# Order of work at the passage from attention to feed-forward in a transformer kernel

## The reference

```python
q = (query @ Wq + bq)   # 16 heads of 32; query = layernorm(x), x is (2, 2048, 512)
k = (key_value @ Wk + bk); v = (key_value @ Wv + bv)   # context (2, 77, 384)
attn = softmax(clip(einsum('bhqd,bhkd->bhqk', q, k) * scale, -CLAMP, CLAMP))
x = x + einsum('bhqk,bhkd->bqhd', attn, v) @ Wo + bo
# feed-forward: U1 (512,128), V1 (128,2048), U2 (2048,128), V2 (128,512)
P = layernorm(x) @ U1
H = gelu(P @ V1 + b1)
x = x + (H @ U2) @ V2 + b2
```

## Time and profile before

| | us |
|---|---|
| median of 3 runs | 556.8 |
| lowest and highest | 556.72, 557.4 |
| the profiled execution | 556.77 |
| its span | 555.0 |
| PE busy | 546.0 (98%) |
| DVE busy | 474.7 (86%) |
| POOL busy | 371.7 (67%) |
| ACT busy | 310.3 (56%) |

### The profile page before, as it was taken

One profiled execution on the slowest core, in us unless ns is written; L12 is line 12 of the kernel. 1 busy time (PEld: TensorE's weight loads), 2 busy tenths in 40 slices (PEclk: granted clock), 3 DMA queues, 4 the chain that ended last, 5 costly groups with the idle time before them and its releaser, 6 DMA issues.

```text
span 555.0 us, 12058 instructions
## 1 busy us (share of the span) xinstructions
PE 546.0 (98%) x4824; PEld 464.6 (84%) x4824; DVE 474.7 (86%) x692; ACT 310.3 (56%) x523; POOL 371.7 (67%) x295
## 2 busy tenths in 40 slices
PE   8999999999999999999999999999999999999996
PEld 8997889888988898889877777888888888888885
DVE  5789989888988898889899568989889898978694
ACT  4655454545554555454455546757575757666563
POOL 1788776778777877786679356747484756565581
PEclk9999999999999999999999999999999999999999
DMA  8432452321223122243322230031221222101012
GB/s 320 173 84 75 122 225 93 97 93 64 94 96 109 49 95 97 89 146 129 134 67 75 71 114 1 19 107 46 63 89 58 76 75 79 57 19 58 20 57 94
DMA packets 25551, 50.36 MB, mean 91 GB/s; under 512 B 2968, under 2 KB 3096, under 8 KB 25112
## 3 DMA queue, kind: packets, MB, share of 16 engines
q1 hardware_dynamic: 25208, 49.07, 26.0%
q10 hardware_dynamic: 288, 0.52, 0.3%
HBM read 32.49 MB, written 16.78 MB: 89 GB/s over the span
## 4 chain that ended last, share of the span: by engine, by line
PE 86%; DVE 7%; POOL 3%; ACT 2%; issue 1%; DVEq 0%; POOLq 0%
PE bank L1044 50%; PE ps_s L1044 15%; PE bank L1122 6%; PE ps_s L1096 5%; PE bank L1138 5%; PE bank L1065 2%; PE bank L1169 2%; DVE once L867 1%; PE bank L1204 1%; DVE ssum L835 1%; POOL wqo_r L411 1%; POOL ss L422 1%; DVE wqo_r L872 1%; DVE hs_r L890 1%; POOL ss L430 1%
## 5 line engine op out<-in xcount | busy, mean ns | idle before, releaser
L513 POOL TENSOR_TENSOR hs_r<-ss,hs_r 128x512 fp32r<-128x512 f32 x63 | 88.2, 1401 | 91.4 <-ACT hs_r L743 91.4
L656 ACT ACTIVATE ss<-ps_s,once 128x512 f32<-128x512 f32 x128 | 88.1, 689 | 65.1 <-PE ps_s L1044 61.6
L1044 PE MATMUL ps_s<-p1t_r,v_r 128*128 128x512 f32 x384 | 111.1, 398 | 0.0
L1044 PE MATMUL bank<-hs_r,u_r 128*128 128x512 f32 x381 | 107.2, 390 | 0.0
L1044 PE MATMUL bank<-zt_r,wqo_r 128*128 128x256 f32 x768 | 97.7, 283 | 0.2 <-ACT qt L544 0.2
L422 POOL TENSOR_TENSOR ss<-ss,smax 128x1232 f32<-128x1232 f32 x32 | 74.8, 2338 | 33.0 <-DVE smax L830 33.0
L1044 PE MATMUL bank<-wqo_r,ot_r 128*128 128x512 f32 x384 | 95.5, 398 | 0.0
L1044 PEld LDWEIGHTS bank<-zt_r,wqo_r 128*128 128x128 f32 x768 | 91.8, 188 | 1.5 <-issue 0.4
L1044 PEld LDWEIGHTS bank<-hs_r,u_r 128*128 128x128 f32 x381 | 71.4, 188 | 15.7 <-DVE hs_r L890 0.2
L1044 PEld LDWEIGHTS bank<-wqo_r,ot_r 128*128 128x128 f32 x384 | 69.8, 188 | 13.5 <-DVE ot_r L843 0.2
L1044 PEld LDWEIGHTS ps_s<-p1t_r,v_r 128*128 128x128 f32 x384 | 69.8, 188 | 13.4 <-issue 0.4
(11 more groups left out here) (97 smaller groups left out, 818.1 us busy)
## 6 DMA issues: line engine op xcount, KB each, us to landing
xs<-in_x SPq DMA_DIRECT2D x64, 256.0 KB, 3.4
y_between<-xs SPq DMA_DIRECT2D x32, 256.0 KB, 2.0
fw<-y_between SPq DMA_DIRECT2D x4, 1024.0 KB, 5.5
xs<-y_between SPq DMA_DIRECT2D x4, 1024.0 KB, 5.4
out<-fw SPq DMA_DIRECT2D x16, 256.0 KB, 2.0
out<-xs SPq DMA_DIRECT2D x16, 256.0 KB, 2.0
xs<-in_Wo SPq DMA_DIRECT2D x1, 1024.0 KB, 8.4
fw<-in_v SPq DMA_DIRECT2D x1, 1024.0 KB, 7.1
```

Source lines behind the costliest of these rows:

```text
L513: pool.tensor_tensor(hs[:, c % 4, 1, :], hg[:, c % 4, :], hs[:, c % 4, 0, :].bitcast(F32), ALU.subtract)\
L656: act.activation(hg[:, c % 4, :], ps_s[:, c % 4, :], ACT.Gelu_apprx_tanh, bias=b1_c[:, c:c + 1]).then_inc(h_gelu, 1)
L1044: mm = pe.matmul(ps, lhs(a), rhs(c), start=first and i == 0, stop=last and i == len(PASSES) - 1)
```

## The change

Only the order in which DVE and ACT work through the passage changes. No instruction is added or taken away; PE's, POOL's and SP's lists stay.

```diff
@@ last_tiles of ACT
                 copy_probs(j, 1, 0, (0, 1, 2))
+                copy_probs(j, 1, 1, (0, 1, 2))
                 gelu(0, 0, 0)
-                copy_probs(j, 1, 1, (0, 1))
                 gelu(0, 0, 1)
-                copy_probs(j, 1, 1, (2,))
@@ last_tiles of DVE
                 sums(j, 0, 0)
-                for t in range(UB):
+                for t in range(UB - 1):
                     norm_z2(0, 0, t)
+                heads_low(j - 1, 1)
                 y_sum(j - 1, 0, 1)
-                heads_low(j - 1, 1)
                 turned_z2(0, 0, 0)
+                norm_z2(0, 0, UB - 1)
                 sums(j, 0, 1)
...
                 sums(j, 1, 0)
+                turned_z2(0, 0, 3)
                 y_sum(j - 1, 1, 1)
-                turned_z2(0, 0, 3)
                 sums(j, 1, 1)
...
                 y_sum(j, 0, 1)
+                norm_z2(0, 1, 0)
+                norm_z2(0, 1, 1)
                 heads_low(j, 1)
                 h_split(0, 0, 2)
+                norm_z2(0, 1, 2)
+                norm_z2(0, 1, 3)
                 y_sum(j, 1, 0)
                 y_sum(j, 1, 1)
@@ DVE, ahead of body2
-            for t in range(UB):
-                norm_z2(0, 1, t)
```

## The result

The changed kernel took 557.75 us as the median of 22 runs (556.97 to 558.2), the kernel before 556.83 in 22 runs beside it. The ratio is 1.0013, with a 95% interval of 1.0007 to 1.0019: slower by 0.4 to 1.1 us, 0.7 in the middle. The forecast was 557.3, 0.5 slower. Here is the page's first line of the changed kernel, and busy time of the passage, as long a stretch as in the earlier trace rows and counted from the same instruction (columns: stretch, its length, busy us of PE, PE's weight loads, DVE, ACT, POOL, granted clock, DMA share, GB/s).

A forecast was written before the change was run, and what follows sets the result against it. PE was taken as the bound, busy 40.34 of 42.16 us in the changed stretch. With earlier steps included, 0.63 won became 0.51 lost, DVE's relief counted 0: 556.77 + 0.51 = 557.3 us, range 555.7 to 558.2.

The forecast's parts named there:

- Step 1: First heads, DVE: fourth norm_z2 moved behind heads_low, y_sum, turned_z2; PE's 0.83 us wait replaced by later waits, DVE 0.18 later.
- Step 2: Ahead of block 0's U1 product: turned_z2(0,0,3) placed before y_sum on DVE; gain 0.07 us, moved y_sum costs nothing.
- Step 3: Last attention tile, ACT: all three copies before the first gelu; PE's 0.63 us wait goes entirely, gelu 2.5 us late.
- Step 4: Block 1's norm_z2 sooner, two before the last heads_low: wait for 1/std turns 0.63 won into 0.51 us lost.
- no gain behind 324: First feed-forward block: moving four norm_z2 saves DVE 1.91 us but gains PE 0, bounds 0 to 0.5.
- The sum: Whole kernel: net +0.51 us on 556.77, giving 557.3 us.
- Faster: Rival: PE keeps the gaps it lost, 0.83 + 0.25 + 0.63 = 1.7 us, so 555.1 us; chance 0.12.
- No net move: Rival: DVE's relief behind 324 gives back 0.5 us at z2's low parts, so 556.8 us; chance 0.14.
- The lock: Rival: four DVE operations beside POOL from about 318.5 lengthen, delaying y_sum; 558.5 or 560.0 us; chance 0.08.
- The table switch: Rival: ACT's table load before the first gelu takes twice its 1.30 us, so 558.6 us; chance 0.06.

The follow-up runs named there:

- step 1 alone: Kernel before, with DVE at the first heads reordered: three norm_z2, heads_low, y_sum, turned_z2, fourth norm_z2; ratio 1.0007, passage 57.37 us.
- step 3 alone: Kernel before, with all three probability copies of the last half-tile ahead of the table load and both gelus; ratio 0.9987, passage 56.38 us.
- steps 1 to 3: Changed kernel with the four norm_z2 of block 1 put back where they were before; ratio 0.9982, passage 56.36 us.
- step 4 alone: Kernel before, with block 1's norm_z2 moved ahead: two before the last heads_low, two behind h_split(0,0,2); ratio 1.0003, passage 57.13 us.

## Why the prediction was right

**Step 1** was right in size and, but for one path, in mechanism. Predicted and found, aligned: turn for the heads 287.45 and 287.46, projection 288.65 and 288.66, next turn 293.95 and 293.84, sums 0.18 and 0.15 later. I had PE held only at that turn, by sums and POOL. It is held mostly one group sooner, by DVE's clip behind the sums: 0.71 from the row at 292.46 to 293.17, against 0.31 before (292.55 to 292.86), and 0.14 at the turn itself (1.21 against 1.07 behind the group ahead of it). That the idle time is the cause is shown by the sums put into it.

**Step 2** was right in its start and missed a follower. The U1 product was to gain 0.07 and gained 0.17. I had read how long PE stood there off the bracket, 0.25; from start to start it was 0.33 (298.56 to 301.33 before, 299.26 to 301.70 after). The follower is the two heads' low parts of tile 14, at 303.78 (303.24 aligned) against 303.09. The projection behind the turn that needs them starts 3.78 us after the U1 product (305.48 - 301.70), against 3.62 before, so 0.16 is lost again. The moved y_sum costs nothing, as I had said: DVE waits 0.26 for ACT's exponent behind it, and with step 1 alone, where y_sum is not moved, the heads' low parts are as late (21.53 us behind the first norm_z2, 21.54 in the changed kernel, 21.39 before). The lateness is step 1's. Held against step 1 alone, step 2 won 0.32 at the U1 product (19.78 to 19.46) and kept 0.16 at the projection (23.40 to 23.24); that makes up for what step 1 lost, and the two together net nothing (23.25 before). The passages say the same: 56.38 with step 3 alone and 56.36 with steps 1 to 3. Step 2 alone was not run.

**Step 3** was right that PE's wait goes and the gelu is about 2.5 us late (312.47 aligned, forecast 312.38). One size was off: the wait I priced at its bracket, 0.63, is worth 0.80. PE's next row starts 0.78 after the hidden group in the changed kernel (310.11 to 310.89) and 1.58 after it before (309.55 to 311.13). The bracket counts from the modelled end of the last matmul, and that reaches beyond the start of a following one (310.11 + 0.95 = 311.06, beside 310.89). It did not change the sum, since the heads decided.

**Step 4** was right in mechanism: project_out(1,0) at 318.83 aligned, forecast 318.83, from 318.32. That the two agree to the hundredth is luck, for two errors cancel. Norm_z2 was at 316.58 (forecast 316.49) and the heads at 317.50 (317.40), since the 0.07 won in step 2 had not lasted; and PE started 1.33 behind the heads' start, not 1.43. The experiments show the mechanism from three sides: with step 4 alone (so without the late gelu, but without steps 1 and 2 too), without the norm_z2 in front, or with the statistics ahead of the split, PE does not wait. The "no gain behind 324" held too: 0.05 came back to the end of the passage (+0.51 to +0.46), and the wait near 332 stayed.

**The sum** was +0.51 on the profiled execution; the passage shows +0.46 and the timing +0.4 to +1.1. The forecast had held 0.2% to be the least that can be told; 22 runs of each told 0.13%. The timing's middle is 0.2 us higher than the trace, which lies within its interval; what such a difference is, if it is one, stays open.

**The rivals.** Faster (555.1): not so, for the reasons given, but about as much as its 1.7 us could be had by another order. The kernels with the sums first are about 1.6 faster than the one before. No net move: close by, excluded by the interval. The lock: DVE's four operations beside POOL took 1.18, 1.66 and 1.96 for two from 319.23 on, 4.8 us in all, under the 5.8 from which it would have decided, and PE did not wait for y. With the heads first it did, by about 0.17. The table switch: the gelu began 1.30 after the load started (311.71 to 313.01), as before. The drain that the Trainium skill, "ScalarE: Activation LUTs", section "What ACT_TABLE_LOAD costs", adds to a switch is in neither trace.

## What to carry to other kernels

An operation moved ahead on an in-order engine takes with it the wait of its own inputs. Before putting it in front of something urgent, follow its inputs back, and look for a step that the same change makes late. Here the chain ran over three engines (ACT's gelu, DVE's split and statistics, POOL's 1/std, and back to DVE), and two steps of one change met on it: one made its start late, the other put its end in front of something urgent. And when a wait is removed from the bounding engine but an idle stretch appears on the one that feeds it, put into that stretch the operation on which the next wait rests. That was worth 0.6 us here.

## What was not expected of the hardware

The bracketed idle time of PE understates what a stall costs: 0.63 shown, 0.80 from start to start, and 0.83 shown against 0.90 at the heads (286.88 to 288.36 before, 287.42 to 288.00 after). Starts are the better ruler.

norm_z2 beside POOL ended about 0.3 us behind the end of POOL's operation. In the kernel with step 4 alone, two from 320.48 took 2.95 us (1.52 and 1.51, the second from 321.9), while POOL ran the two operations below, which end at 321.71 and 323.15. A pair took 1.00 at 316.24, with POOL idle.

```profile
320.42 1.29 POOL L513 TENSOR_TENSOR hs_r<-ss,hs_r 128x512 fp32r<-128x512 f32 x1 [5.17 <-ACT hs_r L743]
321.68 1.47 POOL L503 TENSOR_TENSOR fw<-fw,bias_row 128x512 f32<-128x512 f32 x1
```
